# Four-bit digits, one logit product and a shorter place computation in a routed two-layer kernel

## The reference, cut to what matters

```
flat_x = einsum('bct,bcd->bdt', x, weights[subjects]) as (4096, 256)
logits = flat_x @ Wg + bg                       # 4 experts
top_vals, top_idx = top_k(logits, 2);  probs = softmax(sparse)
for i in range(4):
    score = where(assigned, probs[:, i], -inf)
    sel_p, sel_idx = top_k(score, 1024)
    out.at[sel_idx].add(gelu(flat_x[sel_idx] @ W1[i]) @ W2[i] * p)
x = x + out
x = x + second_layer(x)      # low-rank adapters, SiLU gate, linear; untouched by the change
```

## Time and profile before

| | |
|---|---|
| runs | 598.23 us median of 3 (597.64 to 598.33) |
| profiled execution | 599.74 us, its span 597.9 us |
| TensorE busy | 576.5 us, 96% of the span |
| VectorE, ScalarE, GpSimd busy | 372.3, 241.4, 143.5 us |
| mean granted TensorE clock | 0.985 |
| chain that ended last | PE 90%, DVE 5%, DMA 2% |

### The profile page before, as it was taken

One profiled execution on the slowest core, in us unless ns is written; L12 is line 12 of the kernel. 1 busy time (PEld: TensorE's weight loads), 2 busy tenths in 40 slices (PEclk: granted clock), 3 DMA queues, 4 the chain that ended last, 5 costly groups with the idle time before them and its releaser, 6 DMA issues.

```text
span 597.9 us, 10448 instructions
## 1 busy us (share of the span) xinstructions
PE 576.5 (96%) x3627; PEld 482.0 (81%) x3627; DVE 372.3 (62%) x898; ACT 241.4 (40%) x545; POOL 143.5 (24%) x122
## 2 busy tenths in 40 slices
PE   4987999999999999999999999999999999999996
PEld 2865799899999999987878878878788788787885
DVE  6298866765677556666566564575566655744733
ACT  2254457665864664653422412322324033123110
POOL 3000322563464451656003003021030030100000
PEclk9689899999999999999999999999999999999999
DMA  8987569344339322553004104023041041130012
GB/s 304 339 284 233 193 208 372 57 132 117 36 87 311 46 46 27 113 127 89 9 0 129 23 2 137 14 84 62 5 123 26 0 132 18 36 83 7 10 27 36
DMA packets 64655, 61.06 MB, mean 102 GB/s; under 512 B 37504, under 2 KB 56704, under 8 KB 63264
## 3 DMA queue, kind: packets, MB, share of 16 engines
q1 hardware_dynamic: 53168, 37.97, 21.3%
q0 software_dynamic: 9264, 22.22, 15.2%
q10 hardware_dynamic: 2176, 0.26, 0.3%
HBM read 45.17 MB, written 19.47 MB: 108 GB/s over the span
## 4 chain that ended last, share of the span: by engine, by line
PE 90%; DVE 5%; DMA 2%; SPq 1%; issue 1%; ACT 0%; another core or an unknown queue 0%; DVEq 0%; ACTq 0%
PE bank L1379 25%; PE bank L1381 24%; PE bank L1380 24%; PE bank L1649 5%; PE bank L1607 2%; PE bank L1406 2%; DMA xT<-in_xT 2%; PE bank L1452 1%; PE bank L1499 1%; PE bank L1599 1%; PE bank L1490 1%; PE bank L1616 1%; PE bank L1617 1%; PE bank L1737 1%; PE bank L1464 1%
## 5 line engine op out<-in xcount | busy, mean ns | idle before, releaser
L746 ACT ACTIVATE act<-bank 128x512 f32<-128x512 f32 x64 | 38.2, 599 | 184.2 <-PE bank L1649 174.9
L1335 DVE TENSOR_TENSOR prod<-bank,act 128x512 f32<-128x512 f32 x64 | 44.2, 691 | 97.8 <-PE bank L1649 81.0
L1189 DVE TENSOR_TENSOR hid_lo<-hf,hid_hi 128x512 fp32r<-128x512 f32 (+1 forms) x80 | 46.8, 586 | 53.9 <-ACT hf L669 49.9
L1379 PE MATMUL bank<-w_hi,hid_hi 128*128 128x256 f32 x256 | 71.9, 281 | 0.2 <-DVE hid_lo L1189 0.2
L1380 PE MATMUL bank<-w_lo,hid_hi 128*128 128x256 f32 x256 | 71.4, 279 | 0.0
L1381 PE MATMUL bank<-w_hi,hid_lo 128*128 128x256 f32 x256 | 71.3, 279 | 0.0
L666 ACT ACTIVATE hid_hi<-bank 128x512 fp32r<-128x512 f32 (+1 forms) x80 | 41.2, 515 | 66.7 <-PE bank L1381 55.2
L496 POOL DMA_INDIRECT x_rows<-y_sb,slot_row x32 | 52.6, 1644 | 44.8 <-ACT y_sb L636 32.6
L485 POOL DMA_INDIRECT xg<-flat_rows,slot_row x32 | 36.2, 1132 | 88.4 <-DVE slot_row L1038 45.1
L1379 PE MATMUL bank<-xs_hi,w_hi 128*128 128x512 f32 (+1 forms) x158 | 56.8, 360 | 0.0
L519 POOL DMA_INDIRECT b_pair<-b_rows,b_row x8 | 8.3, 1032 | 200.9 <-PE bank L1697 200.3
(11 more groups left out here) (314 smaller groups left out, 1283.7 us busy)
## 6 DMA issues: line engine op xcount, KB each, us to landing
w_raw<-in_L_ffn_W SPq DMA_DIRECT2D x8, 1024.0 KB
flat_rows<-x_sb SPq DMA_DIRECT2D x8, 520.0 KB, 5.0
xT<-in_xT SPq DMA_DIRECT2D x8, 512.0 KB, 8.7
x_sb<-in_x SPq DMA_DIRECT2D x8, 512.0 KB, 8.1
outT<-out_sb SPq DMA_DIRECT2D x120, 32.0 KB
wdT<-in_wdT SPq DMA_DIRECT2D x1, 1024.0 KB, 5.4
wg_lo_raw<-in_L_cond_Wg SPq DMA_DIRECT2D x1, 1024.0 KB, 6.6
wu_lo_raw<-in_L_cond_Wu SPq DMA_DIRECT2D x1, 1024.0 KB
```

Source lines behind the costliest of these rows:

```text
L746: act.activation(act1[h % 2][:, :], bank[h % 2][:, :], ACT.Silu).then_inc(silu1, 1)
L1189: dve.tensor_tensor(lo[:, n], hf[s % 2][:, n], hi[:, n].bitcast(f32), ALU.subtract).then_inc(hid0, 1)
L1335: dve.tensor_tensor(prod[par][h][:, :], bank[2 + h % 2][:, :], act1[h % 2][:, :], ALU.mult).then_inc(prod1, 1)
L1379: pe.matmul(out, lh, rh, start=start, stop=False, skip_group_check=True)
```

## The change

The digits get four bits, in four steps on each of the two parts (shifts 11, 7, 3, 0: the last digit has three new bits and one that overlaps), with 15 candidates instead of seven. ROWS_FIRST becomes 16, so that the items still add up to 32. The logits are one group of eight products with 128 moving columns behind the last quarter of `z_own`. The polynomial is evaluated in levels. The places come from one running sum over the marked tokens (those above first, then the equal ones), with 4096 added for tokens that carry no mark; the minimum over both marks is the place. `passed`, larger now, lies over `zT`.

```diff
-SEARCH_STEPS, SEARCH_BITS = 10, 3
-HIGH_STEPS, LOW_BITS = 5, 15
+SEARCH_STEPS, SEARCH_BITS = 8, 4
+HIGH_STEPS, LOW_BITS = 4, 15
+SHIFTS = (11, 7, 3, 0)
...
-    restart[:, :, 0] = 0.0
+    restart[:, 0::2, 0] = 0.0
...
-        passed = [sb(f"passed{i}", [P, CAND, G, EH], bf16) for i in range(2)]
...
+        cursor[0] = offset_of["zT"]
+        passed = [sb(f"passed{i}", [P, CAND, G, EH], bf16) for i in range(2)]
+        assert cursor[0] <= offset_of["logit"]
...
-        need = sb("need", [P, E], f32)
+        off = sb("off", [P, E, 2, G], f32)
...
-        ROWS_FIRST = 12
+        ROWS_FIRST = 16
...
-            dve.wait_ge(logit_mm, 4)
+            dve.wait_ge(logit_mm, 1)
...
-            link(dve.tensor_scalar(t_[:, :], r_[:, :], EXP_C[0], None, ALU.mult))
-            for c in EXP_C[1:]:
-                link(dve.scalar_tensor_tensor(t_[:, :], t_[:, :], c, r_[:, :], ALU.add, ALU.mult))
+            done(dve.tensor_tensor(r2[:, :], r_[:, :], r_[:, :], ALU.mult))
+            done(dve.tensor_scalar(top_[:, :], r_[:, :], c7, c6, ALU.mult, ALU.add))
+            done(dve.tensor_scalar(end[:, :], r_[:, :], c3, c2, ALU.mult, ALU.add))
+            link(dve.tensor_scalar(mid[:, :], r_[:, :], c5, c4, ALU.mult, ALU.add))
+            first = done(dve.tensor_tensor(top_[:, :], top_[:, :], r2[:, :], ALU.mult))
+            second = done(dve.tensor_tensor(end[:, :], end[:, :], r2[:, :], ALU.mult))
+            done(dve.tensor_tensor(r4[:, :], r2[:, :], r2[:, :], ALU.mult))
+            dve.wait_ge(chain, first)
+            first = done(dve.tensor_tensor(mid[:, :], mid[:, :], top_[:, :], ALU.add))
+            dve.wait_ge(chain, second)
+            done(dve.tensor_tensor(end[:, :], end[:, :], r_[:, :], ALU.add))
+            dve.wait_ge(chain, first)
+            link(dve.tensor_tensor(mid[:, :], mid[:, :], r4[:, :], ALU.mult))
+            link(dve.tensor_tensor(t_[:, :], mid[:, :], end[:, :], ALU.add))
...
+            dve.wait_ge(ranks_in, 1)
+            link(dve.tensor_scalar(off[:, :, :, :], above[:, :, :, :], -float(TOK), float(TOK), ALU.mult, ALU.add))
             dve.wait_ge(ranked, 1)
...
-                link(dve.tensor_tensor_scan(flat(incl), restart[:, 0:n * 2 * G], counts[:, 1, cs], 0.0, ALU.mult, ALU.add))
-                link(dve.tensor_tensor(flat(prefix), flat(incl), counts[:, 1, cs], ALU.subtract))
-                dve.tensor_scalar(need[:, es], incl[:, es, 0, G - 1], -1.0, float(CAP), ALU.mult, ALU.add)
-                link(dve.tensor_tensor(flat(prefix), flat(prefix), counts[:, 0, cs], ALU.add))
+                i = done(dve.tensor_tensor(flat(prefix), flat(off), counts[:, 0, cs], ALU.add))
+                scanned = done(dve.tensor_tensor_scan(flat(incl), restart[:, 0:n * 2 * G], counts[:, 1, cs], 0.0, ALU.mult, ALU.add))
+                dve.wait_ge(chain, i)
+                done(dve.tensor_tensor(flat(prefix), flat(prefix), counts[:, 1, cs], ALU.subtract))
+                dve.wait_ge(chain, scanned + 1)
+                link(dve.tensor_tensor(flat(prefix), flat(incl), flat(prefix), ALU.add))
-            def chosen(es):
...
             def quarters(es):
+                link(dve.tensor_tensor(pos_i[0][:, es, :], prefix[:, es, 0, :], prefix[:, es, 1, :], ALU.min))
                 dve.tensor_scalar(pos_i[1][:, es, :], pos_i[0][:, es, :], 6, None, ALU.logical_shift_right)
-                link(dve.tensor_tensor(t_eg[0][:, es, :], t_eg[0][:, es, :], above[:, es, 0, :], ALU.add))
-                dve.tensor_scalar(pos_i[0][:, es, :], pos_i[0][:, es, :], R2 - 1, None, ALU.bitwise_and)
-                link(dve.tensor_scalar(t_eg[0][:, es, :], t_eg[0][:, es, :], -64.0, 64.0, ALU.mult, ALU.add))
+                link(dve.tensor_scalar(pos_i[0][:, es, :], pos_i[0][:, es, :], R2 - 1, None, ALU.bitwise_and))
             def positions(es):
-                dve.tensor_copy(pos_r[:, es, :, :], over(pos_i[0][:, es, :], C))
-                link(dve.tensor_tensor(pos_q[:, es, :, :], over(pos_i[1][:, es, :], C), over(t_eg[0][:, es, :], C), ALU.add))
+                dve.tensor_copy(pos_q[:, es, :, :], over(pos_i[1][:, es, :], C))
+                link(dve.tensor_copy(pos_r[:, es, :, :], over(pos_i[0][:, es, :], C)))
...
-            def logits(q):
-                if q == 0:
-                    pe.wait_ge(blocks_in, 1)
-                pe.wait_ge(z_in, q + 1)
-                c = slice(q * G, (q + 1) * G)
-                for a in range(NAD):
-                    last = pe.matmul(bank[6][:, c], subj_block[:, a, :], z_own[:, a, c], start=a == 0, stop=a == NAD - 1)
-                last.then_inc(logit_mm, 1)
             def z_by_token(q):
                 pe.wait_ge(z_ev, q + 1)
                 if q >= 2:
-                    logits(q - 2)
+                    pe.wait_ge(z_in, q - 1)
...
             z_by_token(3)
-            for q in range(2, 4):
-                logits(q)
+            pe.wait_ge(blocks_in, 1)
+            pe.wait_ge(z_in, 4)
+            for a in range(NAD):
+                last = pe.matmul(bank[6][:, 0:P], subj_block[:, a, :], z_own[:, a, :], start=a == 0, stop=a == NAD - 1)
+            last.then_inc(logit_mm, 1)
```

More of the change, by code:

```diff
@@ L57, in shape_constants @@
         "adapter": np.broadcast_to(np.arange(NAD, dtype=np.float32), (P, NAD)),
-        "steps": np.broadcast_to(np.concatenate([np.arange(1, CAND + 1) * 2.0 ** (SEARCH_BITS * (HIGH_STEPS - 1 - i))
+        "steps": np.broadcast_to(np.concatenate([np.arange(1, CAND + 1) * 2.0 ** SHIFTS[i]
                                                  for i in range(HIGH_STEPS)]).astype(np.float32), (P, CAND * HIGH_STEPS)),
@@ L877, in _ @@
             link(dve.scalar_tensor_tensor(r_[:, :], p1[:, :], -LN2_LO, r_[:, :], ALU.mult, ALU.add))
-            link(dve.tensor_scalar(t_[:, :], r_[:, :], EXP_C[0], None, ALU.mult))
-            for c in EXP_C[1:]:
-                link(dve.scalar_tensor_tensor(t_[:, :], t_[:, :], c, r_[:, :], ALU.add, ALU.mult))
+            c7, c6, c5, c4, c3, c2 = EXP_C[:6]
+            top_, mid, end, r2, r4 = p1, p2, rest_, m2, neg
+            done(dve.tensor_tensor(r2[:, :], r_[:, :], r_[:, :], ALU.mult))
[12 more added lines that the diff above has]
+            link(dve.tensor_tensor(t_[:, :], mid[:, :], end[:, :], ALU.add))
             link(dve.scalar_tensor_tensor(t_[:, :], t_[:, :], 1.0, n_i[:, :], ALU.add, ALU.mult))
@@ L1008, in positions @@
             def positions(es):
-                dve.tensor_copy(pos_r[:, es, :, :], over(pos_i[0][:, es, :], C))
-                link(dve.tensor_tensor(pos_q[:, es, :, :], over(pos_i[1][:, es, :], C), over(t_eg[0][:, es, :], C), ALU.add))
-            for part_of in (prefixes, chosen, quarters, positions):
-                part_of(slice(0, 1))
+                dve.tensor_copy(pos_q[:, es, :, :], over(pos_i[1][:, es, :], C))
+                link(dve.tensor_copy(pos_r[:, es, :, :], over(pos_i[0][:, es, :], C)))
@@ L1016, in _ @@
+            first_e = slice(0, 1)
+            prefixes(first_e)
+            quarters(first_e)
+            positions(first_e)
             dve.wait_ge(vals_in, 1)
@@ L1194, in _ @@
                 if s == 3:
-                    chosen(later)
+                    quarters(later)
                 if s == 4:
-                    quarters(later)
-                if s == 5:
                     positions(later)
```

## The result

The change takes 597.33 us (median of 20 runs, 594.91 to 599.40); the kernel before took 599.60 beside it (20 runs; one of them, at 649.26, is left out of the ratio). The ratio is 0.996, 95% interval 0.9942 to 0.9979: some 2.4 us less, where 6.7 had been forecast, and outside the range of 588.8 to 595.2. The profiled execution took 598.04 us with a span of 596.2; before it was 599.74 and 597.9, so its span shows 1.7 less.

The account below looks back on a forecast made before the run. PE was taken to bound up to the logits, VectorE from 29.25 on. The terms -8.3 - 0.1 - 1.0 + 2.5 + 1.0 - 0.8 gave -6.7: 591.5 us on the median of 598.23, range 588.8 to 595.2.

Parts of the forecast that it names:

- Logits, 8.3 less: Logits products on PE: `logit` at 21.0 instead of 29.25, taking the full clock; bounds 8.6 to 3.5 us less.
- rival B: Logits and items on PE: clock falls as before and returns only during the items; +2.4 us, 593.9; chance 0.12.
- Items hidden: The 16 first items on PE start at 21.65 and end at 28.8, hidden before the first question's products at 28.9.
- Softmax: Softmax to first question on VectorE: polynomial 0.1 less, `cand` stall 1.0 less, 1.1 us in all; first question at 28.3.
- Search, 2.5 more and a stall of 1.0: Search from first question to `thr`: eight steps of 2.75 us, 22.7 against 20.17, plus 1.0 for the stall beside `wfT_s`.
- Places, 0.8 less: Places on VectorE, from the minimum to the first one-hot tile: 0.9 us instead of 1.63.
- Behind: From the last stores and first gather on: store margin shrinks by 0.8 from 2.1 us; no gain or loss counted.
- The stores are not the bound: At the first gather: it starts 2.97 us after all stores of rows had landed, so stores do not hold it.
- I take nothing: Two folds on PE behind the routing: at most 1 us to be had at full clock, counted as zero.
- Rival D: At the gather, a store of rows or fixed-time load ends last; up to 5 of 6.7 us lost, 596.5; chance 0.03.
- C: Cheaper rival: scaling falls beside a wait, folds behind routing run at full clock; -0.6 and -1, 589.9; chance 0.13.

Follow-up runs that it names:

- three bits: The changed kernel with the search of before (ten steps of three bits, 12 items first); ratio to the kernel before 0.9969.
- three bits and both loads late: The changed kernel with the ten-step three-bit search and the loads of `wg` and `wu` both behind the first gather; ratio to the kernel before 0.9897.
- the change paced: The changed kernel with `wg` and `wu` loaded behind the first gather and the last two x copies held until the third gather landed; ratio 0.9916.
- logits alone: The kernel before with only the logits edit (one group of eight products behind the last quarter); ratio to the kernel before 0.9937.
- kept busy: The changed kernel with 14 products of 512 columns, results unread, on PE behind the folds; ratio to the kernel before 0.9951.
- load late: The changed kernel with the load of `wu` and the loads behind it issued only when the first gather has landed; ratio to the kernel before 0.9972.
- search alone: The kernel before with only the four-bit search, 16 first items and the place of `passed`; ratio to the kernel before 1.0026.
- both loads late: The changed kernel with the loads of `wg` and `wu` both behind the first gather; ratio to the kernel before 0.9977.

## Why the prediction was wrong

The steps up to the gather were right, the transfers that stand around the gather were priced at nothing, and that step failed.

- **Logits, 8.3 less:** 8.37 in the profile (`logit` at 20.88, forecast 21.0), sixteen records in 2.02 us at a clock of 1.00. But the full clock was one of two cases. The same records ran at 0.53 to 0.57 in four of the other twelve profiles that have them (with three bits, with three bits and both loads late, the change paced, and the logits alone) and took 3.65, 3.62, 3.46 and 3.32. So rival B is an outcome that a single execution of the same front may have, worth 1.3 to 1.6 us there; that this profile had the full clock was luck in part.
- **Items hidden:** right, 28.76 against a first question at 28.53, and its products at 29.23.
- **Softmax:** the first question at 28.53, forecast 28.3.
- **Search, 2.5 more and a stall of 1.0:** `thr` came 24.42 behind the first question, where 23.7 was forecast with the stall. The step (2.75) was exact to 0.03. The two `key_f` operations beside GpSimd took 1.27, where they take 0.35 in the kernel kept busy: a stall of 0.9, forecast 1.0. Most of the 0.7 too little, 0.63, is the fifth step: while VectorE stood in the low keys and the stall, PE idled 2.38 us and the clock fell. The Trainium skill's figure in "TensorE: Matmul & The Clock Gate", section "Back-to-back issue gap", 81 ns for a pair of weight load and product with 128 columns in a sustained stream, doesn't hold for these with 120: at a granted clock of 1.00 eight of them span 0.58 us (32.02 to 32.60), which, less the 0.216 of one, is 0.052 for each next.
- **Places, 0.8 less:** 0.77 between minimum and first one-hot tile, 0.87 from `thr` to `slot_row`.
- **Behind: "The stores are not the bound", "I take nothing":** this step failed. I took for the margin of the stores that of the kernel before, moved by the instructions that issue them, and priced its end at zero. What speaks against it stood in the earlier trace rows, the DMA share: 0.95 from 29 to 37 and 1.00 before it, and I read their clock only. The stores moved with the items (the first leaves at 33.44, where it left at 37.59), into a stretch that the loads already filled, and what waited kept the engines full to 58. The last store, issued 5.2 us earlier, landed 3.3 earlier. The margin, forecast at 1.3 us, was gone: the store landed at 60.76, 0.6 behind the end of `slot_row`. It cost nothing yet at the gather's start (1.04 behind the row numbers, 1.05 before), but it set free `wu`, on whose distance from the gather the 5.98 us hung: rows 2.43 us later after the gather's start than before, and 1.47 of low clock behind PE's wait.

Rival D had the place ("a store of rows in front of it, or a load at a fixed time") and, at 596.5, almost the time: 599.60 - 597.33 = 2.3 less, on 598.23, is 595.9. It got 0.03, for the reason that "SP issues by events that move along". They do, and that was the trouble: the event of `wu` is the last store's landing, which moved by 3.3 us while the gather moved by 6.0. The exclusion of a loss behind the gather made the range too narrow as well; the low clock there, counted as a gain in C, could go either way.

By the Trainium skill, "DMA: Bandwidth & Descriptors", section "Issuing engines are not separate DMA queues", transfers of different issuers run on the same 16 engines and interleave. The trace agrees: the gather beside `wu` took 5.79 us and without it 2.99 to 3.17.

## What to carry to other kernels

When a change brings a stage forward, list each transfer that its first and its next waits depend on, with the issue and landing of whatever stands just ahead in time, and ask for each whether its own trigger moves by as much; read the DMA share of the stretch into which they move. A gain at a gather is worth only what its rows gain, and PE's wait there is paid again in clock. Check the following gathers too, since removing one collision moved the next gather into another that had been hidden.

## What was not expected of the hardware

- With a load of 1 MB (and two of 128 KB behind it) issued 0.26 us ahead of an indirect gather, its first transfer landed 5.8 to 6.5 us after its start (after, kept busy, three bits) instead of 3.2 (load late); with the load 1.06 ahead (logits alone) it was still 5.82 from the gather to the rows. With the load 2.97 and 4.94 ahead (before, search alone) it was 3.5 and 3.4, and there PE came to the rows from its folds without a wait. Beside the copies from HBM to HBM, of 1 MB each, a gather took up to 10.44.
- The landing of the last store followed its issue only in part. In the six profiles whose chain goes through it, issues at 50.98, 51.70, 52.75, 53.00, 53.19 and 53.64 landed at 59.63, 60.33, 60.71, 60.79, 61.51 and 60.76. That `wg`, issued ahead of it, holds it up is borne out by both loads late, where the last store leaves by 53.6, and the DMA share is nothing from 58 on.
- Beside GpSimd's scaling of 512 columns (1.08 us) one small VectorE operation was held until the scaling was over. With the logits alone the scaling ran from 37.63 to 38.71, and `kept` (14 elements, 0.17 alone) from 37.78 to 38.75; with three bits it ran from 38.40 to 39.49, and `kept` from 38.69 to 39.52. Two reductions that began beside it before that, at 38.44 and 38.57, took their usual 0.21 and 0.16.
